# A new order of the work of a part: k and q first, the three tiled products in one run, transposes and v ahead of the next scores

## The reference, cut to what matters

```python
x = L0_attn_x                                  # 4 x 1024 x 256
n = layernorm(x)
q, k, v = n @ W_q.T, n @ W_k.T, n @ W_v.T      # 16 heads of 16
attn = einsum('bihd,bjhd->bhij', q, k) * decay / sqrt(16)   # decay = gamma_h ** (i - j), 0 above the diagonal
y = einsum('bhij,bjhd->bihd', attn, v)
yn = (y - y.mean((1, 3))) / sqrt(y.var((1, 3)) + eps)       # per batch and head, over the whole sequence
x = x + (yn * gn_weight + gn_bias) @ W_o.T
x = x + ffn(layernorm(x))                      # a shared gated FFN and 8 experts of fixed assignment
```

## Time and profile before

| | |
|---|---|
| median of 3 runs | 434.4 us |
| lowest and highest | 433.68 and 434.84 us |
| the profiled execution, time | 434.14 us |
| its span (first to last instruction) | 432.3 us |
| busy: PE, VectorE, ScalarE, GpSimd | 99%, 79%, 49%, 17% of the span |
| granted clock of TensorE over the span | 1.0 |

### The profile page before, as it was taken

The page is one execution under the profiler, slowest core; times in us unless marked ns, Lnnn a source line. Parts: engine busy times, 40 slices in busy tenths (PEclk is TensorE's granted clock), DMA queues, the critical chain, the costliest instruction groups (busy, mean ns, idle before and its releaser), DMA issues.

```text
span 432.3 us, 14448 instructions
## 1 busy us (share of the span) xinstructions
PE 426.3 (99%) x6276; PEld 385.8 (89%) x6276; DVE 339.4 (79%) x803; ACT 210.4 (49%) x403; POOL 74.9 (17%) x69
## 2 busy tenths in 40 slices
PE   7999999999999999999999999999999999999997
PEld 6899999999999999998989988899888999888996
DVE  6888899877987889977798887978879878746423
ACT  3555556445744467445247325473344834346530
POOL 2103323522353122550510000100001000000000
PEclk9999999999999999999999999999999999999999
DMA  8533332232331131225420016000142001120011
GB/s 273 181 112 102 100 102 76 77 110 75 120 98 52 52 117 55 89 94 192 164 84 2 0 50 227 17 0 1 49 155 88 0 1 49 49 97 2 0 50 49
DMA packets 15816, 34.66 MB, mean 80 GB/s; under 512 B 2416, under 2 KB 3088, under 8 KB 15248
## 3 DMA queue, kind: packets, MB, share of 16 engines
q1 hardware_dynamic: 15328, 33.18, 22.6%
q10 hardware_dynamic: 432, 0.66, 0.5%
HBM read 25.44 MB, written 8.40 MB: 78 GB/s over the span
## 4 chain that ended last, share of the span: by engine, by line
PE 98%; DVE 1%; ACT 1%; issue 0%; ACTq 0%
PE bank L379 54%; PE bank L388 13%; PE bank L389 7%; PE bank L457 7%; PE bank L500 4%; PE bank L487 4%; PE bank L471 3%; PE bank L436 2%; PE bank L397 1%; PE bank L647 1%; PE bank L518 1%; PE bank L581 0%; ACT kexp L703 0%; PE bank L512 0%; DVE vexp L1171 0%; DVE xlo L1187 0%
## 5 line engine op out<-in xcount | busy, mean ns | idle before, releaser
L379 PE MATMUL bank<-x2hi,sw_hi 128*128 128x512 f32 x128 | 51.3, 400 | 0.0
L379 PE MATMUL bank<-x2lo,sw_hi 128*128 128x512 f32 x128 | 50.4, 394 | 0.0
L379 PE MATMUL bank<-x2hi,sw_lo 128*128 128x512 f32 x128 | 50.3, 393 | 0.0
L718 ACT ACTIVATE keo<-kT,msk 128x512 f32<-128x512 f32 x32 | 21.4, 715 | 49.4 <-DVE kT L900 49.4
L388 PE MATMUL bank<-w_both,ehi 128*128 128x512 f32 x124 | 44.9, 397 | 0.0
L388 PE MATMUL bank<-sw_both,ghi 128*128 128x512 f32 x124 | 44.8, 394 | 0.0
L911 DVE TENSOR_TENSOR pm<-bank,msk 128x512 f32<-128x512 f32 x64 | 39.8, 682 | 6.4 <-PE bank L457 6.1
L788 ACT ACTIVATE sil<-bank,s1b 128x512 f32<-128x512 f32 x32 | 22.0, 688 | 46.6 <-PE bank L379 46.6
L1076 DVE STREAM_TRANSPOSE x2t<-xl 32x256 f32<-32x256 f32 x96 | 41.8, 436 | 1.7
L379 PE MATMUL bank<-xhi,wqkv_hi 128*128 128x256 f32 x128 | 38.2, 298 | 1.3 <-DVE xlo L895 0.7
L807 ACT ACTIVATE ehi<-xres 128x512 fp32r<-128x512 f32 x32 | 20.2, 633 | 32.9 <-PE bank L389 32.4
(11 more groups left out here) (139 smaller groups left out, 1111.8 us busy)
## 6 DMA issues: line engine op xcount, KB each, us to landing
w_raw<-w SPq DMA_DIRECT2D x16, 256.0 KB, 3.1
xres<-xs SPq DMA_DIRECT2D x16, 256.0 KB, 3.4
x_scratch<-xres SPq DMA_DIRECT2D x16, 256.0 KB, 2.8
xl<-x_scratch SPq DMA_DIRECT2D x8, 512.0 KB, 4.3
xr<-x_scratch SPq DMA_DIRECT2D x4, 1024.0 KB, 4.8
xin<-xa SPq DMA_DIRECT2D x15, 256.0 KB, 2.9
out<-xr SPq DMA_DIRECT2D x7, 512.0 KB, 2.6
sw_raw<-sw SPq DMA_DIRECT2D x6, 256.0 KB, 3.9
```

The lines of the kernel that those rows point to most:

```text
L379: mm = nc.tensor.matmul(o, w[c][l], x[c][r], start=first and c == 0 and j == 0, stop=last and c == n - 1 and j == 2)
L718: cp = nc.scalar.activation(keo[:, :, :, odd, :], kT[:].rearrange("p g (c j) -> p c g j", c=CPS), ACT.Copy, scale=parity[:, odd:odd + 1])
```

## The change

The order of PE's work in a part. Before: sums of part h, k of h+1, q, from the scores, from the state, transposes of k, v, transposes of x of h+2, scores of h+1. After: k of h+1, q, sums of part h, from the scores, from the state, transposes of k, transposes of x, v, scores. `head_vars` moves from behind `from_state` to the place ahead of v. On VectorE `decay_k` moves ahead of `add_state`, `gn_spread` behind `decay_q`, `gn_eps` behind `ln_apply` and the residuals, and `low_y` and `y_sums` from ahead of `ln_apply` to behind `low_x`. `high_x` waits for `v_done` too, as the transposes no longer stand behind v. `high_x(1)` ahead of part 0 moves from ScalarE to VectorE. GpSimd does `ln_power` ahead of `gn_power`. On the DMA queue of SP the loads of the slot biases come behind the load of x. One warm-up matmul at the start is gone. The waits for `pm_ready` ahead of `output_bias` and `output` are gone (before the last part). The last part (h = 15) keeps its order.

```diff
--- before.py
+++ after.py
@@ -27,7 +27,7 @@
 HS, HR = 512, 256
 MS, MR = HS // P, HR // P
 HALF = T // 2
-WARM_UP = (5, 1)
+WARM_UP = (4, 1)
 ORDER = [NE - 1] + list(range(NE - 1))
 
 HIGH_STEPS = (0, 1, 2, 3, 4, 6, 7, 8, 10, 11, 12)
@@ -325,11 +325,6 @@
                 if h == 3:
                     sp.wait_ge(bias_part, 4)
                     sp.dma_start(bias_dram, bias_in[:, 0, :]).then_inc(bias_stored, 16)
-                if h == 10:
-                    sp.wait_ge(bias_stored, 16)
-                if h in (10, 14):
-                    load_slot_bias((h - 10) // 2)
-                    load_slot_bias((h - 10) // 2 + 1)
                 if h + 3 <= PARTS:
                     sp.wait_ge(t_done, h + 4)
                 if h + 6 < PARTS:
@@ -338,6 +333,11 @@
                     load_xl(0, 0)
                 if h == 13:
                     load_xl(0, 1)
+                if h == 10:
+                    sp.wait_ge(bias_stored, 16)
+                if h in (10, 14):
+                    load_slot_bias((h - 10) // 2)
+                    load_slot_bias((h - 10) // 2 + 1)
 
             for h in range(PARTS):
                 step(h)
@@ -529,25 +529,12 @@
 
             def step(h):
                 b, s = h // NSUP, h % NSUP
-                if h == 0:
-                    project_k(1)
-                state_sums(h)
-                if 0 < h < PARTS - 1:
-                    project_k(h + 1)
-                if b and s == 0:
-                    pe.wait_ge(pm_ready, h * PAIRS + 1)
-                    head_means(b - 1, p_bank[0])
-                if h + 1 < PARTS:
-                    project_q(h + 1)
-                else:
-
+                if h + 1 == PARTS:
+
+                    state_sums(h)
                     transpose_x2(0)
                     pe.wait_ge(pm_ready, h * PAIRS + 1)
                     output(b - 1, 2, p_bank[2])
-                if h + 1 < PARTS:
-                    from_scores(h, True)
-                    from_state(h, False)
-                else:
                     from_state(h, True)
                     transpose_x2(1)
                     pe.wait_ge(pm_ready, h * PAIRS + 2)
@@ -556,21 +543,28 @@
                         pe.wait_ge(pm_ready, h * PAIRS + (j + 1))
                         transpose_x2(j)
                     from_scores(h, False)
+                    return
+
+                project_k(h + 1)
+                if b and s == 0:
+                    pe.wait_ge(pm_ready, h * PAIRS + 1)
+                    head_means(b - 1, p_bank[0])
+                project_q(h + 1)
+                state_sums(h)
+                from_scores(h, True)
+                from_state(h, False)
+                if b and s == 1:
+                    output_bias(b - 1, p_bank[1])
+                if b and s >= 2:
+                    for j in range(2 * (s - 2), 2 * (s - 2) + 2):
+                        output(b - 1, j, p_bank[j])
+                k_by_tokens(h + 1)
+                if h + 2 < PARTS:
+                    transpose_x(h + 2)
                 if b and s == 0:
                     head_vars(b - 1, p_bank[0])
-                if b and s == 1:
-                    pe.wait_ge(pm_ready, h * PAIRS + 2)
-                    output_bias(b - 1, p_bank[1])
-                if b and s >= 2 and h + 1 < PARTS:
-                    for j in range(2 * (s - 2), 2 * (s - 2) + 2):
-                        pe.wait_ge(pm_ready, h * PAIRS + (j + 1))
-                        output(b - 1, j, p_bank[j])
-                if h + 1 < PARTS:
-                    k_by_tokens(h + 1)
-                    project_v(h + 1)
-                    if h + 2 < PARTS:
-                        transpose_x(h + 2)
-                    scores(h + 1)
+                project_v(h + 1)
+                scores(h + 1)
 
             def transpose_x2(j):
 
@@ -689,11 +683,6 @@
 
         @block.scalar
         def _(act):
-            def high_x(h):
-
-                act.wait_ge(t_done, h + 2)
-                nc.scalar.activation(xhi[:].rearrange("p c t -> p (c t)"), b_bank[:], ACT.Copy).then_inc(xhi_ready, 1)
-
             def by_heads(dst, bank):
 
                 src = bank[:].rearrange("p (t r h e) -> p t r h e", t=TILES, h=2, e=DH)
@@ -763,6 +752,7 @@
                     copy_bias(b - 1, p_bank[1])
                 if h + 1 < PARTS:
                     copy_k(h + 1)
+                if h + 1 < PARTS:
                     copy_v(h + 1)
                 if h in HIGH_STEPS:
                     high_ffn(HIGH_STEPS.index(h))
@@ -826,7 +816,6 @@
             spread_k(0)
             act.wait_ge(kexp_cleared, 1)
             copy_k(0)
-            high_x(1)
             act.wait_ge(v_cleared, 2)
             copy_v(0)
             for h in range(PARTS):
@@ -888,6 +877,7 @@
             def high_x(h):
 
                 dve.wait_ge(t_done, h + 2)
+                dve.wait_ge(v_done, h)
                 nc.vector.tensor_copy(xhi[:].rearrange("p c t -> p (c t)"), b_bank[:]).then_inc(xhi_ready, 1)
 
             def low_x(h):
@@ -998,11 +988,11 @@
                 b, s = h // NSUP, h % NSUP
                 if h + 1 < PARTS:
                     mask_scores(h, range(PAIRS))
+                    decay_k(h + 1)
                     add_state(h)
+                    decay_q(h + 1)
                     if b and s == 0:
                         gn_spread(b - 1, p_bank[0])
-                    decay_k(h + 1)
-                    decay_q(h + 1)
                     carry_state(h)
                 else:
                     mask_scores(h, (2,))
@@ -1020,8 +1010,6 @@
                     ln2_sums(0, 0)
                 elif h + 2 == PARTS:
                     ln2_sums(0, 1)
-                if b and s == 0:
-                    gn_eps(b - 1, p_bank[0])
                 if h + 1 == PARTS:
                     y_sums(h)
                     gn_channels(b)
@@ -1029,8 +1017,6 @@
                         residual(b - 1, j, p_bank[j])
                     low_y(h)
                     return
-                low_y(h)
-                y_sums(h)
                 if h + 3 < PARTS:
                     ln_apply(h + 3)
                 if b and s >= 2:
@@ -1038,9 +1024,13 @@
                         residual(b - 1, j, p_bank[j])
                 if h + 3 >= PARTS:
                     ln2_apply(0, h + 3 - PARTS)
+                if b and s == 0:
+                    gn_eps(b - 1, p_bank[0])
                 if h + 2 < PARTS:
                     high_x(h + 2)
                     low_x(h + 2)
+                low_y(h)
+                y_sums(h)
                 if s == NSUP - 1:
                     gn_channels(b)
                 if b and s == 0:
@@ -1196,6 +1186,7 @@
             decay_q(0)
             dve.wait_ge(msk_landed, 16)
             ln_sums(2)
+            high_x(1)
             low_x(1)
             ln_apply(2)
             dve.wait_ge(gn_landed, 32)
@@ -1269,12 +1260,12 @@
 
             def step(h):
                 b, s = h // NSUP, h % NSUP
-                if b and s == 0:
-                    gn_power(b - 1)
                 if b and s == 1:
                     spread_bias(b - 1)
                 if h + 3 < PARTS:
                     ln_power(h + 3)
+                if b and s == 0:
+                    gn_power(b - 1)
                 if h + 3 >= PARTS and h + 1 < PARTS:
                     ln2_power(0, h + 3 - PARTS)
 
```

## The result

The change makes the kernel slower: 444.67 us (median of 6 runs, 443.52 to 447.32) against 434.32 us (6 runs, 433.68 to 435.13), a ratio of 1.0245 with an interval of 1.0229 to 1.0262. The direction is the forecast's; the size is not: +10.3 us instead of +2.9, far outside 434.8 to 439.2. The profiled execution took 443.81 us with a span of 442.0 (before: 434.14 and 432.3).

The account below looks back on a forecast made before the run. TensorE (PE), 98% of the chain, was taken to bound the kernel. Gains of 3.0 us (joints, xlo, warm-up) against waits of 5.9 made +2.9 on the profiled 434.14: 437.0 us, range 434.8 to 439.2.

Parts of the forecast that it names:

- The joints: PE, between products of different tiling: 0.58 removed, 0.45 added per part; gain 0.13 to 0.14 in 14 parts, 1.9 us.
- The start: Up to k of part 1: gains of 0.3 at step 0's joints, 0.7 from xlo, 0.1 from the shorter warm-up.
- the wait for xlo: PE ahead of k of part 1: a stand of 0.66 goes, as high_x(1) moves to VectorE.
- 0.1 for the warm-up: Kernel start: one warm-up matmul less gains 0 to 0.34 us, taken as 0.1.
- Wait (a): Parts 5, 9, 13: head_means waits for the mask's first quarter, late behind gn_channels; stall 0.5 us, three times.
- Wait (b): Parts 5, 9, 13: the scores wait for gn_ve, as gn_eps stands behind ln_apply; stall 0.9 us, three times.
- Wait (d): Step 13, ahead of k of part 15: xlo comes late behind ln2_sums and ln2_apply; stall 1.4 us.
- Wait (c): s == 1: gn_affine ahead of the mask makes s_ready 0.07 us too late for from_state, three times.
- (2): Rival: the joint from sums to from_scores costs 0.13 after all, 14 times, 1.8 more; 438.6 us, chance 0.12.
- (3): Rival: s_ready is late for from_state in every plain part, 14 x 0.1 = 1.4 more; 438.4 us, chance 0.10.
- (5): Rival: shorter warm-up leaves TensorE at 1.2 GHz for first projections, up to 1.44 per 12 matmuls; 438.4 us, chance 0.05.
- plain parts show waits at L487: Sign in the changed kernel's profile, at from_state in parts without batch work, that the forecast is wrong.

Follow-up runs that it names:

- e2: Changed kernel with 32 tiny matmuls (128 instructions) ahead of the warm-up and one warm-up matmul less; 449.68 us, ratio 1.0326.
- e9: Changed kernel with 16 tiny matmuls (64 instructions) ahead of the warm-up and one warm-up matmul less; 445.66 us, ratio 1.0241.
- e10: Changed kernel with 48 tiny matmuls (192 instructions) ahead of the warm-up and one warm-up matmul less; 451.61 us, ratio 1.0413.
- e1: Changed kernel with the sums moved back between k and q, so only two tiled products (256 instructions) run in a row; 439.29 us, ratio 1.0093.
- e3: Kernel before with from_state issued twice in a row, making a run of 384 instructions with from_scores; 457.18 us in one execution.
- e5: Kernel before with 512 tiny fp32 matmuls (2048 instructions) on four array tiles in turn, ahead of the first warm-up; 462.60 us.
- e7: Kernel before with high_x(1) moved to VectorE behind ln_sums(2) and four warm-up matmuls instead of five; 433.99 us, ratio 0.9978.
- e8: Changed kernel with PE's order of before, the other engines and the SP queue as changed; 437.73 us, ratio 1.0075.
- e11: Changed kernel with from_state doing only its last two chunks before part 15, a run of 320 instructions; 435.96 us in one execution.
- e4: Kernel before with 512 tiny fp32 matmuls (2048 instructions) on one array tile, ahead of the first warm-up; 488.79 us in one execution.

## Why the prediction was wrong

**The step that failed** is the one in which it counts PE's side of the change: "the number of matmuls stays the same and only the joints move". Each joint was priced; what lies between the joints was taken to cost the same wherever it stands. It doesn't. This term, put at nothing, measured 8.4 us. Before, at most two tiled products follow each other; now three do, 384 instructions in 0.72 + 1.02 + 1.03 = 2.8 us. They are used up at 256 per 1.8 us and come at 256 per 3.5 us or more. On the average of a part there is no shortage: about 602 instructions (301 matmuls and as many loads) in 10.2 us are 256 per 4.3 us. Only a run that outlasts what is in store meets the limit. 602 isn't a multiple of 256, so the run lies elsewhere in its blocks in each part; this is why it is six parts of 15, and why the shifts of e2, e9 and e10 move them. It is shown that the gaps go when the run is cut (e1), come when another run is made as long (e3), follow the position in the stream (e2, e9, e10) and that the supply has this pace (e5). That a packet's late arrival ends each gap of the changed kernel is read from the times of the packets, 2.2 to 2.8 us ahead of PE's going on; it wasn't varied by itself.

**The joints** were right in a plain part: 0.13 (forecast 0.13 to 0.14), sums to `from_scores` at 0 and scores to k at 0.21, as taken. The earlier trace rows were enough for it. By the Trainium skill, TensorEngine Tiling (Array Packing), Key Properties, which the prediction cites, only a change of mode drains; the 12 ns of this joint agree. The forecast counted 14 parts, though, and parts 4, 8 and 12 gained next to nothing: 1.5 instead of 1.9. **The start**: the wait for xlo is gone as forecast, k of part 1 is 1.0 earlier. Where the forecast has 0.1 for the warm-up, the first projection is 0.27 earlier in the one trace, but the transposes now wait 0.50 for their input, and e7 shows no such gain.

**Wait (a)**: 0.5 forecast, 0.52 measured, three times. **Wait (b)**: 0.9 forecast, 0.73 and 0.82 measured, in parts 9 and 13; none in part 5, behind the gap of 1.29 in part 4. A gap ahead of it takes such a wait away, as VectorE goes on meanwhile: in e2, e9 and e10, where part 4 has no gap, (b) is 0.82 or 0.83 in part 5. **Wait (d)**: 1.4 forecast, none measured, behind the 1.54 of part 13; where part 13 has no gap it is 1.2 (e2) and 1.1 (e10), and 0.9 in e1, whose parts are longer. **Wait (c)**, 0.07, was not seen. Together 3.1 instead of 5.9. With the gaps away the working comes out: e1 has 0.8 less in part 0, 14 x 0.18 = 2.5 more in the joints (10.53 against 10.35) and 2.9 of waits, +4.6, and its span is 4.6 longer (436.9 against 432.3; that it fits to the tenth is partly chance, as its first scores also begin 0.3 earlier). That the direction came out in the changed kernel is no proof of the forecast's working: the waits alone, 3.1 against gains of 2.8, would have left no change that can be told.

Slips in the working itself change nothing of this: (b) and (d) add to 4.1, not 4.2; (d)'s upper end is 12.8, not 12.75; the chances of the forecast, (2), (3) and (5) already add to 0.82.

**The rivals**: none of the five holds the cause. (2), (3) and (5) stopped at 438.6 or below; full matmuls start 0.12 apart from the first projection on, so (5) didn't happen. (3), "s_ready late", is the one that a quick look at L487 would seem to confirm; the place of the gaps, behind the 44th matmul and not ahead of the first, rules it out. The prediction did name "plain parts show waits at L487" as the sign that it is wrong.

**Open**: the two gaps in a run of 256 in e8 (and the short ones in e3); 1.0 us in small pieces of the changed kernel; and when the lower clock follows. It did within 1.1 us behind stands of 1.1 to 2.2 us in the traces of e2, e9, e10 and e5, 1.9 us behind one of 1.05 in e11, and behind none of the six gaps, up to 1.7 us, in the trace of the changed kernel. Two of its six executions have a lower mean clock and are 1 to 4 us longer than the rest, but have no trace.

## What to carry to other kernels

Before small matmuls are put into one long run, count their instructions (here two for each recorded matmul: itself and its load) against time: here 256 in 1.8 us was too fast for a supply of 256 in 3.5 us or more: a run of 384 gapped in six parts of 15, one of 320 in three, each in one trace, and a product of large matmuls between them (e1) took all the gaps away. Runs of 256 are not quite safe (e8). A saving of 0.13 per part at the joints isn't worth a run that long. In a trace the sign is idle time inside a group, put down to "issue", with an instruction packet some 2 to 3 us before its end; these gaps move with any shift of the stream, so an edit elsewhere can change which part pays. Look at the clock of every execution too: here a stand of PE could cost another 1.5 us or so behind it.

## What the runs showed of the hardware

- The supply of PE's instructions, with no other DMA traffic, gave 256 per 3.46 to 4.01 us (e5).
- The first tiny matmuls of e5 ran without a long gap for 223 records, 446 instructions. The first packet on the queue of PE's instructions started only as they ended, at 7.95, so that much was in store, less than two packets of 256.
- Tiny fp32 matmuls on one tile of the array cost 53.5 ns per recorded matmul (e4), on four tiles in turn 14 ns from start to start (e5, 32x32 weights and 64 columns instead of 32).
- The granted clock fell in e5 at 11.3, after PE had stood from 8.1 to 10.3. The windows view (length, PE busy, loads busy, then VectorE, ScalarE, GpSimd, the clock):

```profile
8.00:10.00 2.00, 0.11 (x7) 0.00 (x0) 0.00 (x0) 0.00 (x0) 0.00 (x0) 1.00 1.02 369
10.00:12.00 2.00, 1.71 (x101) 1.71 (x104) 0.00 (x0) 0.00 (x0) 0.00 (x0) 0.83 0.18 45
12.00:14.00 2.00, 1.27 (x51) 1.05 (x47) 0.00 (x0) 0.00 (x0) 0.00 (x0) 0.50 0.00 0
...
18.00:20.00 2.00, 1.63 (x108) 1.49 (x100) 0.00 (x0) 0.00 (x0) 0.00 (x0) 0.96 0.03 8
```

0.50 is 1.2 GHz; it lasted to 18.2, and of the 256 matmuls from 13.75, which took 5.88 us, most ran at it. It fell again at 28.4, behind the stand of 2.0 us that ended at 28.15.
- The clock was at 0.50 in one stretch each of the traces of e2, e9, e10 and e11, named with them above, and the work in it took 1.5 to 1.7 us longer than the same work in the changed kernel. In the trace of the changed kernel itself it is 1.0 over the span.
